# Single table rows addressed in bytes, one unit in 44 fetched so in place of one in 64, and the lanes of two chunks in one broadcast

## The chip, the cores and the metric

The kernel runs on one core of a Trainium2 chip. The metric is the device time of one execution in microseconds (us), as the median of several runs. TensorE (PE), VectorE (DVE), ScalarE (ACT), GpSimd (POOL) and SyncE (SP) each work through their own list of instructions and wait for one another by semaphores. SP does no arithmetic here: it only starts transfers (DMAs).

## The reference

One layer of graph attention over 6,250 nodes and 206,250 edges, 128 features each:

```
n_in, n_out = node[recv], node[send]
e_ij   = leaky_relu(concat([n_in, n_out]) @ W_att + b_att)      # slope 0.2
a_ij   = e_ij @ w_alpha
a_exp  = exp(a_ij - segment_max(a_ij, recv)[recv])
alpha  = a_exp / segment_sum(a_exp, recv)[recv]
n_i    = segment_sum(alpha * (n_out @ W_lin + b_lin), recv)
x      = layernorm(node + elu(n_i))
```

`recv` and `send` are the two ends of each edge. Nodes are handled in 49 blocks of 128.

## The kernel before

**Preparation.** A table `qv_table` in HBM gets one row of 257 numbers (1,028 bytes) for each node: 128 for the sender's part of the hidden layer, 128 for its value, and a one. The edges are sorted by receiver in four parts, and cut into *units* of 128 edges whose receivers lie in one block.

**The loop.** A *chunk* is four units (512 edges), and the loop runs over `NCH` = 415 chunks. For each chunk:

- The 128 table rows of each unit's senders are brought to SBUF. For three units, and mostly for the fourth as well, POOL does this: `gather(k)` issues one indirect DMA per unit (L651) into the ring `rows`, which holds `U` = 8 chunks. A slot comes free when the sums of the chunk eight earlier are done (`high_sums_done`).
- The lanes (the receiver of each edge within its block) come by `lanes_of(k)` on SP (L516): one list of 512 bf16 numbers, broadcast to all 128 partitions, into the ring `lanes_all` of four chunks.
- DVE compares the lanes with the partition number (`make_onehot`, L1530), PE makes the hidden layer (`hidden`, L965 and L967), ACT and DVE the slope and the maximum, PE the scores (`mask`, L977 and L978), DVE the running maxima, ACT the exponentials, PE turns the weights (L985) and sums the weighted rows (`unit_sums`, L993), and DVE adds these to the block's sums (L1581). PE works on the hidden layer of chunk k + 4 while it sums chunk k. Beside this, in about the first 330 chunks, the engines sort the next part of the edges.

**Single rows.** The last unit of every sixteenth chunk (`single_no`; chunks 15, 31, ..., 399, 25 in all) is not gathered by POOL. SP fetches its 128 rows one by one, spread over sixteen chunks: in each chunk `fetch_rows(k)` has one `TENSOR_LOAD` of eight row numbers into registers (L564), and then eight DMAs of one row each, at an address from a register (L569). `hidden(k)` waits for all 128 rows. The numbers in `single_at` are made by DVE; they are row numbers times 257.

**The order of SP's list** is plain: for each chunk `lanes_of(k)`, then `besides(k)` (a few loads and stores for the sort), then `fetch_rows(k)`. `lanes_of(k)` waits until the onehot four chunks earlier is done, which frees its place in the ring.

The rows that are printed for SP name its own list as SPq.

Of the kernel before, what the change touches and what calls it, by code (L numbers as in the profile page):

```python
# [5 lines left out]
F32 = mybir.dt.float32  # L6
BF16 = mybir.dt.bfloat16
I32 = mybir.dt.int32
ALU = mybir.AluOpType
ACT = mybir.ActivationFunctionType  # L10
AX_X = mybir.AxisListType.X

P = 128
# [6 lines left out]
def gnn_kernel(nc, x, src, dst, w_lin, b_lin, w_att, b_att, w_alpha, out):  # L20
# [5 lines left out]
    CHUNK = C * P  # L26
    PER = 4
    UNIT = P
    U = 8
    R = 2 * F + 1  # L30
# [10 lines left out]
    PAD_ROW = NB * P  # L41
# [13 lines left out]
    NO = KEPT // PER  # L55
# [10 lines left out]
    NCH = sum(NCHS)  # L66
# [34 lines left out]
    LANE_RING = 4  # L101


    ROWS_EACH = 8
    ROW_CHUNKS = -(-UNIT // ROWS_EACH)
    RING_S = 2
    COUNTS_S = 4
    def run_ends_of(s):
# [51 lines left out]
    for k in range(NCH):  # L160
# [4 lines left out]
        if k in boundary_at:  # L165
            for kind in ("group", "lows", "old"):
                s = boundary_at[k]
# [6 lines left out]
    TABLE_LAST = [24]  # L174

    table = nc.dram_tensor("qv_table", [(NB + 1) * P, R], F32, kind="Internal").ap()
    flat_table = table.rearrange("n r -> (n r)")
    pads_dram = nc.dram_tensor("pads", [P, PC], F32, kind="Internal").ap()
    sorted_dram = [nc.dram_tensor(f"windows{s}", [WINDOWS, UNIT], F32, kind="Internal").ap() for s in range(OPEN)]
    lanes_dram = [nc.dram_tensor(f"lane_list{s}", [P * W], BF16, kind="Internal").ap() for s in range(SETS)]  # L180

    with ExitStack() as ctx:
# [6 lines left out]
        def sem(name):  # L189
            return ctx.enter_context(nc.semaphore(name))  # L190
# [6 lines left out]
        onesf = sb("onesf", [P, P], F32)  # L197
        part_i = sb("part_i", [P, 1], I32)
        bit_i = sb("bit_i", [P, 1], I32)
        row_sign = sb("row_sign", [P, 1], F32)  # L200
# [11 lines left out]
        sums = sb("sums", [P, NB, F + 1], F32)  # L212
        single_at = sb("single_at", [P, 2, UNIT], I32)
        single_rows = sb("single_rows", [P, RING_S, R], F32)

        keys_i = sb("keys", [P, 2, W], I32)
        keys = keys_i[:].bitcast(F32)
        rows_of = sb("rows_of", [P, W], F32)
        kept = sb("kept", [P, W], F32)
        columns = sb("columns", [P, W], F32)  # L220
        bits = sb("bits", [P, W], I32)
        lane_rows = sb("lane_rows", [P, W], BF16)
        senders = sb("senders", [P, 2, W], I32)
        blocks = sb("blocks", [P, KEPT], I32)
# [53 lines left out]
        lanes_all = sb("lanes_all", [P, LANE_RING, CHUNK], BF16)  # L278
# [4 lines left out]
        rows = sb("rows", [P, U, C, R], F32)  # L283
# [38 lines left out]
        kept_i = kept[:].bitcast(I32)  # L322
# [44 lines left out]
        lanes_made = sem("lanes_made")  # L367
        lanes_ready = sem("lanes_ready")
        lanes_stored = [sem(f"lanes_stored{s}") for s in range(SETS)]
        lanes_in = [sem(f"lanes_in{r}") for r in range(LANE_RING)]  # L370
        unpacked = sem("unpacked")
        blocks_ready = sem("blocks_ready")
        cleared = sem("cleared")
# [20 lines left out]
        onehotT_ready = sem("onehotT_ready")  # L394
# [59 lines left out]
        def place(k):  # L454

            s = min(k // NO, OPEN)
            return s, k - BEGIN[s]
# [4 lines left out]
        def _(sp):  # L462
# [16 lines left out]
            for g in range(PAIRS):  # L479
                n = min(2, NB - 2 * g)  # L480
# [28 lines left out]

            def lanes_of(k):  # L510
                s, n = place(k)
                if k >= LANE_RING:
                    sp.wait_ge(onehotT_ready, k - LANE_RING + 1)
                if n == 0:
                    sp.wait_ge(lanes_stored[s], 16)
                sp.dma_start(lanes_all[:, k % LANE_RING, :],  # L516
                             lanes_dram[s][n * CHUNK:(n + 1) * CHUNK].rearrange("(a e) -> a e", a=1).to_broadcast([P, CHUNK])
                             ).then_inc(lanes_in[k % LANE_RING], 16)

            def besides(k):  # L520
                if k == RAW_AT:
# [30 lines left out]
            def fetch_rows(k):  # L552

                n = k // ROW_CHUNKS
                if n not in single_of:
                    return
                s, row = place(single_of[n])
                first = k % ROW_CHUNKS * ROWS_EACH
                if first == 0:
                    sp.wait_ge(single_ready, s + 1)  # L560
                    if n >= RING_S:
                        sp.wait_ge(high_sums_done, single_of[n - RING_S] + 1)
                for r in range(first, min(first + ROWS_EACH, UNIT), 8):
                    starts = nc.values_load_multi_w_load_instructions(  # L564
                        single_at[row:row + 1, s % 2, r:r + 8], engines=(mybir.EngineType.SP,), min_val=0,
                        max_val=(PAD_ROW + P - 1) * R,
                        skip_runtime_bounds_check_because="they are rows of the table, times the length of a row")[1]
                    for i in range(8):
                        sp.dma_start(single_rows[r + i:r + i + 1, n % RING_S, :],  # L569
                                     flat_table[bass.ds(starts[i], R)].rearrange("(a r) -> a r", a=1)  # L570
                                     ).then_inc(fetched_in(n)[0], 16)

            sp.wait_ge(qv_stored[0], 16 * (PAIRS - PAIRS // 2))
            sp.wait_ge(qv_stored[1], 16 * (PAIRS // 2))
            sp.wait_ge(pad_rows_stored, 16)
            for k in range(NCH):
                lanes_of(k)
                besides(k)
                fetch_rows(k)

# [14 lines left out]
        def _(pool):  # L595
# [7 lines left out]
            for t, one in ((identf, 1.0), (other, 0.0)):  # L603
                g.affine_select(out=t[:], in_=t[:], compare_op=ALU.not_equal, fill=one, base=0,
                                pattern=[[-1, P]], channel_multiplier=1).then_inc(consts, 1)
# [5 lines left out]
            for at in (low, high):  # L611
                g.tensor_tensor(bias_f[at, :], bias_f[at, :], bias_parts[at, :], ALU.subtract).then_inc(bias_split, 1)
            pool.wait_ge(bias_split, 3)
# [464 lines left out]
        def _(dve):  # L1078
            v = nc.vector
# [16 lines left out]
            dve.wait_ge(consts_v, 4)  # L1096
            v.tensor_scalar(row_sign[:], bit_i[:], -2.0, 1.0, ALU.mult, ALU.add).then_inc(consts_v, 1)

# [118 lines left out]
            def find_lanes(s):  # L1217

                if s:
                    dve.wait_ge(lanes_stored[s - 1], 16)  # L1220
                if s < OPEN:
                    dve.wait_ge(kept_in[s], 16)
                    v.tensor_scalar(bits[0:NO, :], kept_i[0:NO, :], SENDER_BITS, P - 1, ALU.arith_shift_right,
                                    ALU.bitwise_and).then_inc(lanes_made, 1)
                    dve.wait_ge(lanes_made, s + 1)
                    v.tensor_copy(lane_rows[0:NO, :], bits[0:NO, :]).then_inc(lanes_ready, 1)
                    if s >= 2:
                        dve.wait_ge(*fetched_in(max(n for k, n in single_no.items() if place(k)[0] == s - 2)))
                    v.tensor_scalar(single_at[0:NO, s % 2, :], kept_i[0:NO, (PER - 1) * UNIT:PER * UNIT], (1 << SENDER_BITS) - 1,
                                    None, ALU.bitwise_and).then_inc(single_found, 1)  # L1230
                    dve.wait_ge(single_found, s + 1)
                    v.tensor_scalar(single_at[0:NO, s % 2, :], single_at[0:NO, s % 2, :], float(R), None,
                                    ALU.mult).then_inc(single_ready, 1)
                else:
                    dve.wait_ge(aside_out, aside_no["rows", s])
                    v.tensor_scalar(kept_i[:], rows_i[:], (1 << SENDER_BITS) - 1, None, ALU.bitwise_and).then_inc(lanes_made, 1)
                    v.tensor_scalar(bits[:], rows_i[:], SENDER_BITS, P - 1, ALU.arith_shift_right,
                                    ALU.bitwise_and).then_inc(lanes_made, 1)
                    dve.wait_ge(lanes_made, s + 1)
                    v.tensor_scalar(lane_rows[:], kept_i[:], float(PAD_ROW), float(P), ALU.is_ge, ALU.mult).then_inc(lanes_made, 1)  # L1240
                    dve.wait_ge(lanes_made, s + 3)
                    v.tensor_tensor(lane_rows[:], lane_rows[:], bits[:], ALU.add).then_inc(lanes_ready, 1)
                    dve.wait_ge(*fetched_in(max(n for k, n in single_no.items() if place(k)[0] == s - 2)))
                    v.tensor_scalar(single_at[:, s % 2, :], kept_i[:, (PER - 1) * UNIT:PER * UNIT], float(R), None,
                                    ALU.mult).then_inc(single_ready, 1)

            def columns_of(s):
# [232 lines left out]
            for run in range(1, runs_of(0)):  # L1480
# [3 lines left out]
                if run % 2:  # L1484
                    stages = phase - LOCAL
                    for h in (0, 1):
                        side = [keys[:, n, h * PIECE:(h + 1) * PIECE] for n in (now, 1 - now)]
                        dve.wait_ge(turn_out, 2 * (run - 1) + h + 1)
                        for n in range(stages):
                            if n:  # L1490
                                dve.wait_ge(compared[0], done)
                            end = n == stages - 1
# [4 lines left out]
                    if run == runs_of(0) - 1:  # L1497
                        dve.wait_ge(run_done[0], 2 * runs_of(0))
                        now = (now + stages) % 2
                        for stage in range(LOCAL - 1, UNIT_BITS - 1, -1):  # L1500
                            if stage < LOCAL - 1:
                                dve.wait_ge(compared[0], done)
                            end = stage == UNIT_BITS
# [20 lines left out]


            def make_onehot(k):
                dve.wait_ge(lanes_in[k % LANE_RING], (k // LANE_RING + 1) * 16)
                if k >= 4:
                    dve.wait_ge(masked_done, k - 3)
                v.tensor_scalar(onehotT[:, k % 4, :], lanes_all[:, k % LANE_RING, :], part_f[:], None, ALU.is_equal, ALU.add,  # L1530
                                accum_out=lane_counts[:, k % 4:k % 4 + 1]).then_inc(onehotT_ready, 1)
# [122 lines left out]
            for g in range(SLICES):  # L1654
                at = slice(g * BY, (g + 1) * BY)
                n = sums[:, at, 0:F]
# [55 lines left out]
```

## Time and profile before

| | |
|---|---|
| median of 3 runs | 2277.44 us (2276.98 to 2277.66) |
| profiled execution | 2278.64 us; from its first instruction to its last 2276.9 us |
| busy | PE 78%, DVE 81%, ACT 65%, POOL 70% of the span |
| DMA | 294 MB, mean 129 GB/s |

Busy shares are averages over the whole span, and issuing a DMA on SP is not counted as busy time of any engine; on POOL it is, since an indirect DMA there is an instruction of the engine.

### The profile page before, as it was taken

What the parts mean: (1) busy time and instruction counts of PE and PEld (TensorE: products, weight loads), DVE (VectorE), ACT (ScalarE), POOL (GpSimd) and SP (SyncE); (2) the same over time, 40 slices, a digit from 0 to 9 for tenths busy, and PEclk for the clock granted to TensorE, in tenths of its full rate; (3) what the DMA queues carried; (4) which work ended last, traced back from release to release, by engine and by line L of the source; (5) the groups of instructions that cost most, each with busy time, mean ns of one, the idle gap of its engine ahead of it and who ended that gap; (6) DMA issues with size and microseconds to landing.
All of it is one profiled execution on the core that took longest, in us unless ns stands there. A gap on an engine that the chain in (4) does not pass through costs nothing.

```text
span 2276.9 us, 63415 instructions
## 1 busy us (share of the span) xinstructions
PE 1779.8 (78%) x11705; PEld 1440.8 (63%) x11705; DVE 1854.8 (81%) x5629; ACT 1471.6 (65%) x4913; POOL 1599.3 (70%) x1670
## 2 busy tenths in 40 slices
PE   5648798888878988887888878888788788877780
PEld 2336676666666766666666666666666666666660
DVE  9849998887789988887898888888767677667667
ACT  2326688876667766665666766676666666666655
POOL 2067777777777777777777777777777777777760
PEclk9869999999999999999999999999999999999995
DMA  3145555555555555555555555555555555555531
GB/s 122 61 113 138 136 138 136 132 133 140 128 135 132 138 133 135 132 138 130 135 132 132 132 138 134 132 136 133 135 137 136 133 137 134 136 134 136 134 105 57
DMA packets 165722, 294.16 MB, mean 129 GB/s; under 512 B 40002, under 2 KB 110014, under 8 KB 165329
## 3 DMA queue, kind: packets, MB, share of 16 engines
q0 software_dynamic: 78864, 216.03, 36.8%
q1 hardware_dynamic: 85733, 73.82, 12.6%
q14 instruction: 292, 2.39, 0.4%
q8 instruction: 101, 1.65, 0.3%
q10 hardware_dynamic: 732, 0.27, 0.1%
HBM read 278.95 MB, written 11.02 MB: 127 GB/s over the span
## 4 chain that ended last, share of the span: by engine, by line
POOL 23%; issue 13%; PE 8%; DVE 5%; DMA 4%; DVEq 1%; ACT 0%; POOLq 0%; ACTq 0%
POOL rows L651 23%; DMA rows<-qv_table,senders 4%; PE hidden_ps L967 2%; PE turned_ps L993 2%; PE masked_ps L978 2%; DVE sums L1581 1%; PE hidden_ps L965 1%; DVE leaky L1537 1%; PE turned_ps L985 1%; DVEq L1581 1%; PE masked_ps L977 0%; DVEq L435 0%; DVE spare L1672 0%; DVE x_sb L1667 0%; DVE keys L1145 0%
## 5 line engine op out<-in xcount | busy, mean ns | idle before, releaser
L651 POOL DMA_INDIRECT rows<-qv_table,senders x1635 | 1571.5, 961 | 498.9 <-issue 471.5
L993 PEld LDWEIGHTS turned_ps<-rows,spare 128*128 128x128 f32 x3270 | 441.8, 191 | 351.3 <-ACT spare L778 207.9
L965 PE MATMUL hidden_ps<-identf,rows 128*128 128x128 f32 x1635 | 461.7, 282 | 257.2 <-DMA rows<-qv_table,senders 242.0
L1581 DVE SCALAR_TENSOR_TENSOR sums<-sums,shrink,turned_ps 128x129 f32 x1660 | 572.7, 345 | 81.4 <-issue 38.4
L763 ACT ACTIVATE spare<-masked_ps,peaks 128x128 f32<-128x128 f32 x1660 | 474.4, 369 | 227.1 <-DVE peaks L1559 225.6
L967 PE MATMUL hidden_ps<-onehotT,p_unit 128*128 128x128 f32 x3320 | 592.4, 280 | 0.0
L993 PE MATMUL turned_ps<-rows,spare 128*128 128x129 f32 x3270 | 481.8, 279 | 114.5 <-DVE sums L1581 108.1
L967 PEld LDWEIGHTS hidden_ps<-onehotT,p_unit 128*128 128x128 f32 x3320 | 523.6, 198 | 0.9 <-issue 0.9
L1544 DVE TENSOR_REDUCE lows<-masked_ps 128x4 f32<-128x512 f32 x415 | 285.6, 688 | 275.9 <-PE masked_ps L978 274.7
L746 ACT ACTIVATE p_unit<-p_all 128x128 f32 x1660 | 400.5, 311 | 74.5 <-issue 50.8
L753 ACT ACTIVATE sloped<-hidden_ps 128x512 f32<-128x512 f32 x415 | 248.9, 600 | 282.8 <-PE hidden_ps L967 278.5
L978 PE MATMUL masked_ps<-leaky,w_cols 128*128 128x512 f32 x830 | 427.5, 596 | 0.0
L965 PEld LDWEIGHTS hidden_ps<-identf,rows 128*128 128x128 f32 x1635 | 237.4, 145 | 298.7 <-issue 283.6
L1530 DVE TENSOR_SCALAR_CACHE_REDUCE onehotT<-lanes_all,part_f 128x512 f32<-128x512 bf16 x415 | 306.8, 739 | 16.3 <-DMA lanes_all<-lane_list 16.0
L1537 DVE TENSOR_TENSOR leaky<-hidden_ps,sloped 128x512 f32<-128x512 f32 x415 | 283.9, 684 | 0.5
L985 PE MATMUL turned_ps<-identf,spare 128*128 128x128 f32 x1660 | 254.9, 277 | 0.0
L778 ACT ACTIVATE spare<-turned_ps 128x512 f32<-128x512 f32 x415 | 247.6, 597 | 4.6 <-PE turned_ps L985 4.3
L1144 DVE TENSOR_TENSOR keys<-keys 128x256 f32<-128x256 f32 (+2 forms) x501 | 195.8, 391 | 14.8 <-ACT keys L700 5.9
L985 PEld LDWEIGHTS turned_ps<-identf,spare 128*128 128x128 f32 x1660 | 201.1, 145 | 0.5 <-issue 0.5
L1145 DVE TENSOR_TENSOR keys<-keys 128x256 f32<-128x256 f32 (+2 forms) x501 | 193.5, 386 | 0.0
L978 PEld LDWEIGHTS masked_ps<-leaky,w_cols 128*128 128x128 f32 x830 | 159.6, 192 | 21.1
L977 PE MATMUL masked_ps<-onehotT,other 128*128 128x512 bf16 x415 | 163.7, 394 | 5.5 <-DVE leaky L1537 5.4
(202 smaller groups left out, 896.5 us busy)
## 6 DMA issues: line engine op xcount, KB each, us to landing
lanes_all<-lane_list SPq DMA_DIRECT2D x415, 128.0 KB
single_rows<-qv_table SPq DMA_DIRECT2D x3200, 1.0 KB
rows<-qv_table,senders POOLq DMA_INDIRECT x1635
qv_table<-rows SPq DMA_DIRECT2D x24, 257.0 KB, 2.7
out<-x_sb SPq DMA_DIRECT2D x1, 1344.0 KB
out<-x_sb SPq DMA_DIRECT2D x1, 896.0 KB
kept<-windows SPq DMA_DIRECT2D x3, 208.0 KB
out<-x_sb SPq DMA_DIRECT2D x1, 448.0 KB
```

What stands on the lines that cost most here:

```text
L651: g.indirect_dma_start(out=rows[:, k % U, c, :], out_offset=None, in_=table, in_offset=bass.IndirectOffsetOnAxis(ap=senders[:, s % 2, c * ...
L746: last = a.activation(p_unit[:, k % 2, c * F:(c + 1) * F], p_all[:, bass.ds(of[c], F)], ACT.Copy)
L763: last = a.activation(weightsT[:, k % 2, unit], masked_ps[:, k % 2, unit], ACT.Exp, bias=peaks[:, at + 2 * n:at + 2 * n + 1])
L965: t.matmul(whole[:, unit], rows_at_unit(k, c)[:, 0:F], identf[:], is_transpose=True, start=True, stop=False, skip_group_check=True)
L967: mm = t.matmul(whole[:, unit], p_unit[:, k % 2, unit], onehotT[:, k % 4, unit], start=False, stop=True, skip_group_check=True)
L978: t.matmul(whole, w_cols[:], leaky[:, k % 2, :], start=False, stop=True).then_inc(masked_done, 1)
L985: mm = t.transpose(weights_ps[:, c * P:(c + 1) * P], weightsT[:, k % 2, c * P:(c + 1) * P], identf[:])
L993: mm = t.matmul(unit_sums_ps[:, c, :], weights[:, k % 2, c * P:(c + 1) * P], rows_at_unit(k, c)[:, F:R], start=True, stop=True)
L1530: v.tensor_scalar(onehotT[:, k % 4, :], lanes_all[:, k % LANE_RING, :], part_f[:], None, ALU.is_equal, ALU.add, accum_out=lane_counts[:, k ...
L1537: v.tensor_tensor(leaky[:, k % 2, :], hidden_ps[:, k % 2, :], sloped[:, k % 2, :], ALU.max).then_inc(leaky_ready, 1)
L1544: v.tensor_reduce(lows_at[:, n * PER:(n + 1) * PER, 1], masked_ps[:, k % 2, :].rearrange("p (i e) -> p i e", i=PER), AX_X, ALU.max, negate ...
L1581: v.scalar_tensor_tensor(out=at, in0=at, scalar=shrink[:, k % 4, i:i + 1], in1=unit_sums_ps[:, i, :], op0=ALU.mult, op1=ALU.add).then_inc( ...
```

## The change

Three things change together. (1) The table is viewed as bytes, `single_at` holds row numbers times 1,028, and each single row is a DMA of 1,028 one-byte elements. (2) A unit is fetched singly every 11 chunks (chunks 10, 21, ..., 406, 37 in all); its 16 loads of eight rows are spread over 11 chunks by `LOADS_TO`, as 1, 1, 2, 1, 2, 1, 2, 1, 2, 1, 2. (3) `lanes_of(k)` runs for even k alone and brings the lanes of two chunks; it waits until the onehot of chunk k - 3 is done, and there are two semaphores of lanes in place of four.

```diff
-    ROW_CHUNKS = -(-UNIT // ROWS_EACH)
+    ROW_CHUNKS = 11
+    LOADS_TO = [-(-UNIT // ROWS_EACH) * n // ROW_CHUNKS for n in range(ROW_CHUNKS + 1)]
...
-    flat_table = table.rearrange("n r -> (n r)")
+    BYTES = R * 4
+    table_bytes = table.bitcast(U8).rearrange("n r -> (n r)")
...
             def lanes_of(k):
                 s, n = place(k)
+                m = min(2, NCH - k)
                 if k >= LANE_RING:
-                    sp.wait_ge(onehotT_ready, k - LANE_RING + 1)
+                    sp.wait_ge(onehotT_ready, k - LANE_RING + m)
                 if n == 0:
                     sp.wait_ge(lanes_stored[s], 16)
-                sp.dma_start(lanes_all[:, k % LANE_RING, :],
-                             lanes_dram[s][n * CHUNK:(n + 1) * CHUNK].rearrange("(a e) -> a e", a=1).to_broadcast([P, CHUNK])
-                             ).then_inc(lanes_in[k % LANE_RING], 16)
+                sp.dma_start(lanes_all[:, k % LANE_RING:k % LANE_RING + m, :].rearrange("p m e -> p (m e)"),
+                             lanes_dram[s][n * CHUNK:(n + m) * CHUNK].rearrange("(a e) -> a e", a=1).to_broadcast([P, m * CHUNK])
+                             ).then_inc(lanes_in[k // 2 % (LANE_RING // 2)], 16)
...
-                first = k % ROW_CHUNKS * ROWS_EACH
+                first, end = [ROWS_EACH * n for n in LOADS_TO[k % ROW_CHUNKS:k % ROW_CHUNKS + 2]]
...
-                for r in range(first, min(first + ROWS_EACH, UNIT), 8):
+                for r in range(first, end, ROWS_EACH):
...
-                    for i in range(8):
-                        sp.dma_start(single_rows[r + i:r + i + 1, n % RING_S, :],
-                                     flat_table[bass.ds(starts[i], R)].rearrange("(a r) -> a r", a=1)
+                    for i in range(ROWS_EACH):
+                        sp.dma_start(single_rows[r + i:r + i + 1, n % RING_S, :].bitcast(U8),
+                                     table_bytes[bass.ds(starts[i], BYTES)].rearrange("(a r) -> a r", a=1)
                                      ).then_inc(fetched_in(n)[0], 16)
...
             for k in range(NCH):
-                lanes_of(k)
+                if k % 2 == 0:
+                    lanes_of(k)
                 besides(k)
                 fetch_rows(k)
...
-                    v.tensor_scalar(single_at[0:NO, s % 2, :], single_at[0:NO, s % 2, :], float(R), None,
+                    v.tensor_scalar(single_at[0:NO, s % 2, :], single_at[0:NO, s % 2, :], float(BYTES), None,
                                     ALU.mult).then_inc(single_ready, 1)
```

The first place is SP's list in the middle of the loop. Before, it repeats one chunk: the lanes, one load, and eight rows, each with an operation on a register ahead of it (moves between registers are not listed here, in either kernel).

```order
L516 DMA lanes_all<-lane_list 128x512
L564 TENSOR_LOAD single_at
L569 REGISTER_ALU
L569 DMA single_rows<-qv_table 1x257
L569 REGISTER_ALU
L569 DMA single_rows<-qv_table 1x257
```

Of the change, SP's list from the lanes of one pair of chunks to those of the next, where three loads stand between them (x8 are eight DMAs in a row).

```order
L520 DMA lanes_all<-lane_list 128x1024
L568 TENSOR_LOAD single_at
L573 DMA single_rows<-qv_table 1x1028 x8
L568 TENSOR_LOAD single_at
L573 DMA single_rows<-qv_table 1x1028 x8
L568 TENSOR_LOAD single_at
L573 DMA single_rows<-qv_table 1x1028 x8
L520 DMA lanes_all<-lane_list 128x1024
```

The operations on registers are gone from between the rows; the lanes stand once for two chunks, with two or three loads behind them in place of one load behind each. In all there are 592 loads and 4,736 rows where there were 400 and 3,200, and 208 broadcasts where there were 415.

The second place is POOL's list of the loop: the gathers (L651) with the scatters of the sort (L633) between them. Before:

```order
L633 DMA windows<-rows_of,place_i 512x128 x4
L651 DMA rows<-qv_table,senders 128x257 x351
L633 DMA windows<-rows_of,place_i 512x128 x4
L651 DMA rows<-qv_table,senders 128x257 x346
L633 DMA windows<-rows_of,place_i 512x128 x4
L651 DMA rows<-qv_table,senders 128x257 x938
```

Of the change:

```order
L638 DMA windows<-rows_of,place_i 512x128 x4
L656 DMA rows<-qv_table,senders 128x257 x348
L638 DMA windows<-rows_of,place_i 512x128 x4
L656 DMA rows<-qv_table,senders 128x257 x344
L638 DMA windows<-rows_of,place_i 512x128 x4
L656 DMA rows<-qv_table,senders 128x257 x931
```

Twelve gathers have left POOL's list (1,635 before, 1,623 now); nothing else in it moved.

## Rows read from the trace of the kernel before

**Rows 1.** The page: busy time of the engines, and the chain that ended last.

```profile
PE 1779.8 (78%) x11705; PEld 1440.8 (63%) x11705; DVE 1854.8 (81%) x5629; ACT 1471.6 (65%) x4913; POOL 1599.3 (70%) x1670
...
POOL 23%; issue 13%; PE 8%; DVE 5%; DMA 4%; DVEq 1%; ACT 0%; POOLq 0%; ACTq 0%
```

**Rows 2.** POOL's gathers, line L651: duration, and what ended the idle time before.

```profile
L651 POOL DMA_INDIRECT rows<-qv_table,senders x1635: 942/949/1577, 129.9 to 2209.3; - x182
...
  issue: 471.5, 1545
  PE turned_ps L993: 27.1, 89
```

**Rows 3.** Timeline of POOL, 1500 to 1520 us: start, length, instruction.

```profile
1500.11 0.95 POOL L651 DMA_INDIRECT rows<-qv_table,senders  x1 [0.30 <-PE turned_ps L993]
...
1519.06 0.95 POOL L651 DMA_INDIRECT rows<-qv_table,senders  x1 [0.30 <-issue]
```

**Rows 4.** SP's waits from 138.2 to 2120 us: total, times, longest.

```profile
SPq L516 <- DVE onehotT L1530: 140.4, 154, 4.6
SPq L537 <- DVE keys L1125: 24.7, 3, 12.0
SPq L546 <- DVE pad_out L1381: 12.2, 1, 12.2
SPq L502 <- DVE lane_rows L1242: 3.9, 1, 3.9
SPq L490 <- DMA windows<-rows_of,place_i: 1.2, 1, 1.2
```

**Rows 5.** SP's instructions by line: shortest/median/longest ns, first and last start.

```profile
L564 SPq TENSOR_LOAD <-single_at x400: 686/727/1059, 138.6 to 2116.4; - x134
L569 SPq ALU_OP  x3200: 32/33/51, 139.4 to 2120.0; - x189
L569 SPq MOVE single_rows<-qv_table x3200: 29/29/42, 139.5 to 2120.1; - x189
L569 SPq DMA_DIRECT2D single_rows<-qv_table x3200: 224/228/312, 139.5 to 2120.1; - x189
L516 SPq DMA_DIRECT2D lanes_all<-lane_list x415: 319/358/363, 138.2 to 2189.3; - x139
```

**Rows 6.** Timelines of SP: the loop's start, its middle, a DMA of the sort, its end.

```profile
138.18 0.36 SPq L516 DMA_DIRECT2D lanes_all<-lane_list  x1
...
1013.21 3.03 SPq L569 DMA_DIRECT2D single_rows<-qv_table  x8
1013.66 0.23 SPq L569 DMA_DIRECT2D single_rows<-qv_table  x1
1016.01 0.23 SPq L569 DMA_DIRECT2D single_rows<-qv_table  x1
1016.29 0.36 SPq L516 DMA_DIRECT2D lanes_all<-lane_list  x1
1017.59 3.03 SPq L569 DMA_DIRECT2D single_rows<-qv_table  x8
...
1027.73 4.78 SPq L496 DMA_DIRECT2D firsts<-windows  x1
...
2120.66 28.09 SPq L516 DMA_DIRECT2D lanes_all<-lane_list  x7
```

**Rows 7.** Busy time of each engine from 1700 to 2200 us.

```profile
core 0: us, PE busy (x) PEld busy (x) DVE busy (x) ACT busy (x) POOL busy (x), PEclk, DMA share, GB/s
...
1700.00:2200.00 500.00, 401.99 (x2752) 331.25 (x2752) 343.31 (x1013) 318.93 (x1118) 378.27 (x400) 0.99 0.53 135
```

**Rows 8.** A DMA's issue with its time to landing; PE's last hidden layer.

```profile
qv_table<-rows SPq DMA_DIRECT2D x24, 257.0 KB, 2.7
...
2213.73 0.27 PE L965 MATMUL hidden_ps<-identf,rows 128*128 128x128 f32 x1
```

**Rows 9.** DVE's waits for lanes over the whole span: total, times, longest.

```profile
DVE onehotT L1530 <- DMA lanes_all<-lane_list: 16.0, 5, 3.9
```

More of the change, by code:

```diff
@@ L8 @@
 I32 = mybir.dt.int32
+U8 = mybir.dt.uint8
 ALU = mybir.AluOpType
@@ L369, in gnn_kernel @@
         lanes_stored = [sem(f"lanes_stored{s}") for s in range(SETS)]
-        lanes_in = [sem(f"lanes_in{r}") for r in range(LANE_RING)]
+        lanes_in = [sem(f"lanes_in{r}") for r in range(LANE_RING // 2)]
         unpacked = sem("unpacked")
@@ L562, in fetch_rows @@
                         sp.wait_ge(high_sums_done, single_of[n - RING_S] + 1)
-                for r in range(first, min(first + ROWS_EACH, UNIT), 8):
+                for r in range(first, end, ROWS_EACH):
                     starts = nc.values_load_multi_w_load_instructions(
-                        single_at[row:row + 1, s % 2, r:r + 8], engines=(mybir.EngineType.SP,), min_val=0,
-                        max_val=(PAD_ROW + P - 1) * R,
-                        skip_runtime_bounds_check_because="they are rows of the table, times the length of a row")[1]
-                    for i in range(8):
-                        sp.dma_start(single_rows[r + i:r + i + 1, n % RING_S, :],
-                                     flat_table[bass.ds(starts[i], R)].rearrange("(a r) -> a r", a=1)
+                        single_at[row:row + 1, s % 2, r:r + ROWS_EACH], engines=(mybir.EngineType.SP,), min_val=0,
+                        max_val=(PAD_ROW + P - 1) * BYTES,
+                        skip_runtime_bounds_check_because="they are rows of the table, times the bytes of a row")[1]
+                    for i in range(ROWS_EACH):
+                        sp.dma_start(single_rows[r + i:r + i + 1, n % RING_S, :].bitcast(U8),
+                                     table_bytes[bass.ds(starts[i], BYTES)].rearrange("(a r) -> a r", a=1)
                                      ).then_inc(fetched_in(n)[0], 16)
@@ L1243, in find_lanes @@
                     dve.wait_ge(*fetched_in(max(n for k, n in single_no.items() if place(k)[0] == s - 2)))
-                    v.tensor_scalar(single_at[:, s % 2, :], kept_i[:, (PER - 1) * UNIT:PER * UNIT], float(R), None,
+                    v.tensor_scalar(single_at[:, s % 2, :], kept_i[:, (PER - 1) * UNIT:PER * UNIT], float(BYTES), None,
                                     ALU.mult).then_inc(single_ready, 1)
@@ L1526, in make_onehot @@
             def make_onehot(k):
-                dve.wait_ge(lanes_in[k % LANE_RING], (k // LANE_RING + 1) * 16)
+                dve.wait_ge(lanes_in[k // 2 % (LANE_RING // 2)], (k // LANE_RING + 1) * 16)
                 if k >= 4:
```

## The prediction

> **What bounds the kernel now.** I read the page first: no engine is over 81% busy, so no mean share names the bound, but the chain that ended last runs through POOL and its issue gaps more than through anything else [rows 1]. So POOL's gathers come next. There are 1,635 of them from 129.9 to 2209.3 us, and the idle time before them is put down to "issue", 1,545 times, which is POOL's own gap; PE's sums, which free a place in the ring, are behind 27 us alone [rows 2]. The timeline shows the even step: from 1500.11 to 1519.06 us lie 15 gathers, 1.26 us each with one longer one among them; 0.95 busy and 0.30 of gap make 1.25 [rows 2, 3]. 1,635 x 1.254 = 2050 of the 2080 us of the loop. POOL runs without a rest: the loop's pace is 4 x 1.254 = 5.02 us a chunk, and 3.76 in each sixteenth.
>
> The second question is how much room SP has, since the change gives SP more. SP's issues are not in the busy shares, so I go to its timeline. One chunk in the middle goes from the first row at 1013.21 to the first row of the next at 1017.59, 4.38 us, with the lanes' DMA only 0.05 us behind the last row, so without any wait [rows 6]. Over the whole loop: the first lanes are issued at 138.18 and those of chunk 400 at 2120.66 us, 1982.5 us for 400 chunks with 400 loads [rows 6]; of these SP waited 182.4 us in all [rows 4], and about 20 went to the sort's other DMAs (one of them 4.78 [rows 6], most about 0.4). That leaves 1780 us, 4.45 a chunk. So SP issues for nine tenths of the time, and its wait is mostly the short one for the onehot that frees a lanes slot [rows 4]. **SP stands 0.5 us a chunk behind POOL's pace as the next bound.**
>
> **What the change costs, part by part.**
>
> *POOL* loses 12 gathers, 12 x 1.254 = 15.0 us. If nothing else becomes the bound the time is 2277 - 15 = 2262. PE has the room for it: 402 us busy in 500 with about 100 chunks, 4.0 us a chunk against 4.88 at the new pace (43 gathers in 11 chunks, 53.9 us) [rows 7].
>
> *SP's price of a row.* From the second row's start (1013.66) to the eighth's (1016.01) are six steps, 0.392 us a row [rows 6]. In it lie three instructions: the operation on a register 0.033, a move 0.029, the DMA's issue 0.228, together 0.290 [rows 5]; 0.102 is between them. The order shows the operation gone. The move I expect to stay: it bears the DMA's own tile names, which the operation does not, it stands once to each such DMA, and lanes, whose address is fixed, have none [rows 5]. So the change saves 0.033 at least and 0.067 with a third of the gaps. I take 0.06, close to the second, since an instruction that is gone can leave no gap of its own. A byte type in place of four bytes changes nothing in the bytes that move, and I cost it at nothing; an issue that gets shorter or longer with it is among the rivals.
>
> *SP's price of a load with its eight rows.* 4.45 less the lanes' 0.40 (0.36 and a gap [rows 5, 6]) is 4.05; less 8 x 0.06 it is 3.57. The `TENSOR_LOAD` in it, 0.727 [rows 5], stays. There are 592 loads in place of 400.
>
> *Lanes.* 208 issues in place of 415. An issue that fills 128 partitions costs 0.36 [rows 5]; with twice the bytes and the same 128 pieces I take the same 0.40 with its gap. That it doubles is the upper bound: 204 x 0.36 = 73 us more in the case where SP is the bound.
>
> *SP in sum.* In 11 chunks 16 x 3.57 + 5.5 x 0.40 = 59.3 us, 5.39 a chunk. POOL needs 4.90 for the same chunk (53.9 / 11). **SP becomes the bound**, by half a microsecond in each of 407 chunks. The two prices cross where a load costs (53.9 - 2.2) / 16 = 3.23, that is where a row gets cheaper by 0.10, half as much again as the operation on the register with its gap.
>
> When SP is the bound nothing makes it wait: POOL runs up to eight chunks ahead, the lanes' slots are free early (the wait of 140 us goes), and the waits for the sort, which arise because SP is ahead of DVE, shrink. So its end is a plain sum from 138.2: 592 x 3.57 = 2113; 204 broadcasts up to chunk 406, 82; other DMAs 20; together 2353. The last rows land some 2.7 us later, if they take as long as the table's stores [rows 8]. Then eight chunks remain, whose gathers POOL has done; they go at PE's pace, 4.2 us (its 4.0 busy and a little) [rows 7], 34 us, to the last hidden layer. Before, that layer began at 2213.7 and the span ended at 2276.9, 63 us later [rows 8], and nothing in that end changes. 2353 + 3 + 34 + 63 = 2453 for the span. The profiled execution took 1.7 us beside its span and was 1.2 above the median, so the median is 2453, 176 us (7.7%) longer.
>
> *The shorter lead of the lanes.* A pair is now asked for one chunk later than its first half was. DVE waited for lanes five times before, 16 us in all [rows 9], so there is a lead; where SP is the bound the lanes come late because SP is late, which is in the sum already.
>
> *The pieces of a row.* An issue that makes 128 pieces takes 0.358 us and one of a single row 0.228 [rows 5], so a piece more costs some 0.001 to issue. The Trainium skill ("DMA: Bandwidth & Descriptors", Why a DMA increments its semaphore by 16 and not by 1) has a DMA split over as many engines, up to 16, as divide its slowest dimension, as the instruction carries it; 257 is prime, 1,028 divisible by 4. By this rule a row addressed in bytes might go as four pieces of 257 bytes, and no row here shows whether it does. By the price of a piece, four in place of one add 0.003 us to a row, 4,736 x 0.003 = 14 us: 2467 in place of 2453. I go by one piece, and keep 2467 among the rivals.
>
> **The rivals.**
>
> *POOL stays the bound, faster.* A row on SP would have to cost 0.29 or less, 0.10 less than now. The mechanism is that the move goes as well: both instructions and two thirds of the gaps, 0.13, make the load 3.01 and SP's chunk 4.58 us, under 4.90. For it speaks that the move may serve the computed offset rather than the DMA; against it that it bears the DMA's names. Then the 12 gathers are the whole difference: 2262, or 2268 where single chunks find their rows late. From 0.10 a row it decides for faster.
>
> *In between.* A row that gets cheaper by 0.07 to 0.10 puts SP between both: 2270 to 2410. In the narrow place where SP costs just what POOL saves, the time is the same.
>
> *Worse than forecast.* The bare 0.033 saved makes the load 3.79 and the time 2581. The same side holds a broadcast whose issue doubles (2526) and, close by, the row in four pieces (2467).
>
> **How the numbers follow.** SP the bound at a price of a row of 0.325 to 0.345: chance 0.66; the load is then 3.51 to 3.67, the time 2418 to 2512, likeliest 2453. POOL the bound: 0.22, at 2262 to 2268. In between: 0.08, of which 0.03 ends as no change. Worse: 0.04. What a measurement of this kernel can tell from no change is about 0.2%, 5 us. Faster 0.23, same 0.03, slower 0.74. The range has to hold 8 in 10, and the likeliest case alone holds 0.66, so it reaches down to the faster one: 2260, and up to 2500, which leaves out the worst and the upper end of the likeliest. The likeliest one's own range is 2410 to 2500.
>
> **What would show it.** Right: in SP's instructions by line no operation but still one move to each row, a step of about 0.33 us between rows, no wait of SP for the onehot, and DVE's onehots or PE's hidden layers waiting for lanes and single rows; chunks of 5.4 us up to chunk 406 and of about 4.2 behind it; POOL waiting for PE's sums in each chunk. Wrong: no move, or a step under 0.29; then SP still waits for the onehot, and POOL's gathers follow one another at 1.25 us to the end.

## The result, and the profile after

The changed kernel takes 2410.66 us (median of 5 runs, 2407.67 to 2411.76) against 2276.98 us of five runs of before: a ratio of 1.0592, 95% interval 1.058 to 1.0604, so 5.9% slower, 134 us. The forecast was 2453, slower, in a range of 2260 to 2500, with 2410 to 2500 as the likeliest case's own. Of the runs below, the medians and ratios leave out one execution of the kernel with 32 row numbers to a load, which took 2586.88 us at a mean granted clock of 0.65 of TensorE, against 0.93 in its others.

The page of the changed kernel, the busy times and the chain that ended last, answers to [rows 1].

```profile
PE 1838.8 (76%) x11705; PEld 1501.1 (62%) x11705; DVE 1848.8 (77%) x5629; ACT 1470.6 (61%) x4913; POOL 1586.4 (66%) x1658
...
SPq 53%; issue 13%; DVE 4%; PE 3%; DVEq 1%; DMA 1%; ACT 0%; ACTq 0%
SPq L573 37%; SPq L568 14%; SPq L520 2%; DVE sums L1586 1%; PE hidden_ps L972 1%; PE masked_ps L983 1%; PE turned_ps L998 1%; DVE leaky L1542 1%; DVEq L1586 0%; DMA lanes_all<-lane_list 0%; PE hidden_ps L970 0%; PE turned_ps L990 0%; DVE spare L1677 0%; SPq L499 0%; DVE x_sb L1672 0%
```

No engine has a larger share than before, and nothing in the busy shares says why the kernel is slower. The chain does: POOL's gathers, 23% of the span before, are gone from it, and 53% of the span is SP's own list, the rows (L573), the loads of row numbers (L568) and the lanes (L520).

SP's instructions by line, shortest/median/longest in ns, first and last start, answer to [rows 5].

```profile
L568 SPq TENSOR_LOAD <-single_at x592: 684/790/1400, 140.0 to 2309.0; - x198
L573 SPq MOVE single_rows<-qv_table x4736: 29/29/42, 140.8 to 2312.1; - x198
L573 SPq DMA_DIRECT2D single_rows<-qv_table x4736: 224/228/505, 140.8 to 2312.2; - x198
L520 SPq DMA_DIRECT2D lanes_all<-lane_list x208: 319/360/376, 139.6 to 2330.4; - x104
```

The operation on a register is gone and the move is there, once to each row. A broadcast of twice the bytes takes 360 ns to issue where one took 358.

Timelines of SP: its first lanes, eight rows of one load with the second and the eighth of them by themselves, the next broadcast and rows, and the end of its loop; they answer to [rows 6].

```profile
139.59 0.36 SPq L520 DMA_DIRECT2D lanes_all<-lane_list  x1
...
506.89 2.52 SPq L573 DMA_DIRECT2D single_rows<-qv_table  x8
507.25 0.23 SPq L573 DMA_DIRECT2D single_rows<-qv_table  x1
509.18 0.23 SPq L573 DMA_DIRECT2D single_rows<-qv_table  x1
509.46 0.36 SPq L520 DMA_DIRECT2D lanes_all<-lane_list  x1
510.69 2.52 SPq L573 DMA_DIRECT2D single_rows<-qv_table  x8
...
2306.42 6.00 SPq L573 DMA_DIRECT2D single_rows<-qv_table  x16
2312.47 18.20 SPq L520 DMA_DIRECT2D lanes_all<-lane_list  x4
```

Six steps from 507.25 to 509.18 are 0.322 us a row; it was 0.392 before. The rows end 192 us later than before, when the last of them was issued just ahead of 2120.66 [rows 6].

Who waits: SP's own waits from 139.6 to 2312 us, then POOL's, DVE's and PE's over the span (total, times, longest); they answer to [rows 2, 4, 9]. The last line is POOL's wait for PE in the kernel before.

```profile
SPq L520 <- DVE onehotT L1535: 1.8, 6, 0.3
SPq L541 <- DVE keys L1130: 0.7, 1, 0.7
...
POOL rows L656 <- issue: 471.3, 1493, 4.3
POOL rows L656 <- PE turned_ps L998: 169.8, 130, 5.9
...
DVE onehotT L1535 <- DMA lanes_all<-lane_list: 260.3, 118, 6.2
PE hidden_ps L970 <- DMA single_rows<-qv_table: 84.5, 34, 4.3
...
POOL rows L651 <- PE turned_ps L993: 27.1, 89, 0.3
```

SP waited 182 us in its loop before, and now waits 2.5 us in 2173: it is saturated. DVE waits 260 us for lanes, 16 before, and PE 84 us for single rows, 34 times, with 37 chunks that have such a unit. POOL waits up to 5.9 us for PE to free a slot of its ring, 0.3 at most before.

### The profile page after: what moved, and what is told of

Same layout as the page of the kernel before. It is cut to its first block, busy times and chain, and to the rows that moved or that the text cites. A ratio compares the mean times of both kernels' runs of the same rounds, so it can differ in the third digit from the quotient of the medians.

```text
span 2410.0 us, 63272 instructions
## 1 busy us (share of the span) xinstructions
PE 1838.8 (76%) x11705; PEld 1501.1 (62%) x11705; DVE 1848.8 (77%) x5629; ACT 1470.6 (61%) x4913; POOL 1586.4 (66%) x1658
## 3 DMA queue, kind: packets, MB, share of 16 engines
q1 hardware_dynamic: 58997, 75.39, 10.7%
## 4 chain that ended last, share of the span: by engine, by line
SPq 53%; issue 13%; DVE 4%; PE 3%; DVEq 1%; DMA 1%; ACT 0%; ACTq 0%
SPq L573 37%; SPq L568 14%; SPq L520 2%; DVE sums L1586 1%; PE hidden_ps L972 1%; PE masked_ps L983 1%; PE turned_ps L998 1%; DVE leaky L1542 1%; DVEq L1586 0%; DMA lanes_all<-lane_list 0%; PE hidden_ps L970 0%; PE turned_ps L990 0%; DVE spare L1677 0%; SPq L499 0%; DVE x_sb L1672 0%
## 5 line engine op out<-in xcount | busy, mean ns | idle before, releaser
L998 PE MATMUL turned_ps<-rows,spare 128*128 128x129 f32 x3246 | 506.6, 284 | 343.6 <-DVE sums L1586 338.4
L972 PE MATMUL hidden_ps<-onehotT,p_unit 128*128 128x128 f32 x3320 | 628.6, 292 | 0.0
L972 PEld LDWEIGHTS hidden_ps<-onehotT,p_unit 128*128 128x128 f32 x3320 | 547.6, 207 | 0.9 <-issue 0.9
L983 PE MATMUL masked_ps<-leaky,w_cols 128*128 128x512 f32 x830 | 439.9, 612 | 0.0
L970 PEld LDWEIGHTS hidden_ps<-identf,rows 128*128 128x128 f32 x1623 | 243.9, 150 | 103.9 <-issue 80.9
L990 PE MATMUL turned_ps<-identf,spare 128*128 128x128 f32 x1660 | 269.2, 288 | 0.0
L990 PEld LDWEIGHTS turned_ps<-identf,spare 128*128 128x128 f32 x1660 | 214.6, 152 | 1.1 <-issue 1.1
L983 PEld LDWEIGHTS masked_ps<-leaky,w_cols 128*128 128x128 f32 x830 | 166.5, 201 | 23.8
L982 PE MATMUL masked_ps<-onehotT,other 128*128 128x512 bf16 x415 | 169.9, 409 | 8.6 <-DVE leaky L1542 8.4
```

The costliest lines, as they stand in the source:

```text
L970: t.matmul(whole[:, unit], rows_at_unit(k, c)[:, 0:F], identf[:], is_transpose=True, start=True, stop=False, skip_group_check=True)
L972: mm = t.matmul(whole[:, unit], p_unit[:, k % 2, unit], onehotT[:, k % 4, unit], start=False, stop=True, skip_group_check=True)
L983: t.matmul(whole, w_cols[:], leaky[:, k % 2, :], start=False, stop=True).then_inc(masked_done, 1)
L990: mm = t.transpose(weights_ps[:, c * P:(c + 1) * P], weightsT[:, k % 2, c * P:(c + 1) * P], identf[:])
L998: mm = t.matmul(unit_sums_ps[:, c, :], weights[:, k % 2, c * P:(c + 1) * P], rows_at_unit(k, c)[:, F:R], start=True, stop=True)
```

## Experiments

Three theories were on record before them. **A**: SP's issues are the bound; the time is the sum of what SP issues up to the last single row, and about 98 us behind it (2410.0 - 2312.5). **B**: the pair of lanes is asked for a chunk later, and DVE's wait for lanes is the cause, not the sign. **C**: the many small transfers hold up the others on the DMA engines. In the diffs the changed kernel is the base.

**Every 16 chunks again**, with bytes and pairs.

```diff
-    ROW_CHUNKS = 11
+    ROW_CHUNKS = 16
```

> The changed kernel with a unit fetched singly every 16 chunks again; bytes and pairs of lanes stay. Theory A (SP's issues are the bound): SP's chunk is one load at 3.50 us (mean of the changed kernel) and half a broadcast at 0.40, 3.70 us, well under POOL's 4.94, and POOL's list is that of before: 2277 us, no change. Theory B (the pair of lanes is asked for a chunk later and DVE waits for it): the pairs are still there, so most of the 134 us stays, over 2350 us. Theory C (the transfers of many single rows hold up the others): as before in number, so 2277 us too.

Measured: 2275.36 us against 2274.64 of before on the same chip, ratio 1.0003 (0.9994 to 1.0012), no change. The pairs alone cost nothing, against B. SP's waits from 140 to 2117 us show where the cheaper issues went, into SP's wait:

```profile
SPq L520 <- DVE onehotT L1535: 457.7, 173, 7.4
```

**Every 13 chunks.**

```diff
-    ROW_CHUNKS = 11
+    ROW_CHUNKS = 13
```

> The changed kernel with a unit fetched every 13 chunks: 31 units, six gathers fewer than before. Theory A: SP's chunk is 16 x 3.50 / 13 + 0.20 = 4.51 us, under POOL's (51 gathers x 1.254) / 13 = 4.92, so POOL is the bound and the time is 2277 - 6 x 1.254 = 2269.5 us. Theory B: over 2350 us. Theory C: 768 rows more than before, half of the 1,536 that cost 134 us, so about 2340 us.

Measured: 2266.89 us against 2274.64 of before on the same chip, ratio 0.9964 (0.995 to 0.9977): 7.75 us less where A said 7.5. 768 rows more than before cost nothing as transfers, against C.

**One chunk's lanes in a broadcast**, every 11 chunks.

```diff
-                m = min(2, NCH - k)
+                m = 1
...
-                if k % 2 == 0:
-                    lanes_of(k)
+                lanes_of(k)
```

(with four semaphores of lanes, as before)

> The changed kernel with one chunk's lanes in a broadcast, as before; bytes and a unit every 11 chunks stay. Theory A: SP issues 203 broadcasts more up to chunk 406, 0.40 us each, 81 us: 2492 us. Theory B: the lead is that of before, so the loss goes: 2262 to 2300 us. Theory C: 2410 us, since the lanes' bytes are the same.

Measured: 2479.55 us (one run), 69 us more than the changed kernel, 12 short of A's sum. The lead of before is back and the kernel is slower, not faster: B falls. The loads account for about that: 394 of them stand right behind lanes in place of 199, where a load is some 0.08 us shorter (last section), 15 us in all. This run does not settle C: the lanes' bytes are the same, but they come in 207 broadcasts more, with 29,808 packets more on SP's queue. The next two experiments leave the packets as they are.

**Rows in four-byte elements**, every 11 chunks, with pairs.

```diff
-                        sp.dma_start(single_rows[r + i:r + i + 1, n % RING_S, :].bitcast(U8),
-                                     table_bytes[bass.ds(starts[i], BYTES)].rearrange("(a r) -> a r", a=1)
+                        sp.dma_start(single_rows[r + i:r + i + 1, n % RING_S, :],
+                                     flat_table[bass.ds(starts[i], R)].rearrange("(a r) -> a r", a=1)
```

(and `single_at` times 257)

> The changed kernel with rows addressed in four-byte elements as before, so with the operation on a register ahead of each row; pairs and a unit every 11 chunks stay. Theory A: a load costs 4.05 us (mean of before) in place of 3.50, 592 x 0.55 = 326 us more: 2736 us. Theories B and C: the same transfers and the same lead, so about 2410 us.

Measured: 2760.69 us (one run), 350 us more, 25 above A's sum. SP's instructions by line of this kernel:

```profile
L573 SPq ALU_OP  x4736: 32/33/54, 140.6 to 2661.9; - x198
L573 SPq MOVE single_rows<-qv_table x4736: 29/29/42, 140.7 to 2662.0; - x198
```

The operation alone, 33 ns, is 156 us over 4,736 rows; 350 / 4,736 = 0.074 us is what one cost with its gap. The transfers have not changed: SP's queue has 58,997 packets and 75.39 MB in both kernels.

**Each DMA brings one row to two partitions**, so 64 DMAs to a unit. The kernel leaves out the odd rows of single units and has copies of the even ones in their place, so its output is not that of the layer; its list of work is otherwise the same.

```diff
-                    for i in range(ROWS_EACH):
-                        sp.dma_start(single_rows[r + i:r + i + 1, n % RING_S, :].bitcast(U8),
-                                     table_bytes[bass.ds(starts[i], BYTES)].rearrange("(a r) -> a r", a=1)
+                    for i in range(0, ROWS_EACH, 2):
+                        sp.dma_start(single_rows[r + i:r + i + 2, n % RING_S, :].bitcast(U8),
+                                     table_bytes[bass.ds(starts[i], BYTES)].rearrange("(a r) -> a r", a=1).to_broadcast([2, BYTES])
```

(and the count that `hidden` waits for is halved)

> The changed kernel, every 11 chunks, but each DMA brings one row to two partitions, so 64 in place of 128 of them to a unit; the odd rows of single units are copies of the even ones, their own are left out. The transfers keep their number of pieces and their bytes. Theory A: SP's load falls from 3.50 by 4 x 0.33 to 2.17 us, its chunk to 3.36, under POOL's 4.90: POOL is the bound and the 12 gathers are saved, 2275 - 15 = 2260 us. Theory C: the same pieces, so about 2410 us.

Measured: 2262.18 us against 2277.26, ratio 0.9935 (0.992 to 0.995): 15.1 us less, the 12 gathers and nothing else. This is the cleanest answer to C. Queue of SP (packets, MB, share) of this kernel; in the changed kernel packets and bytes are the same to the digit.

```profile
q1 hardware_dynamic: 58997, 75.39, 11.4%
```

**Every 12 chunks**, where A has SP and POOL level.

```diff
-    ROW_CHUNKS = 11
+    ROW_CHUNKS = 12
```

> The changed kernel with a unit every 12 chunks: 34 units, nine gathers fewer than before. Theory A (SP's issues against POOL's): SP's chunk is 16 x 3.50 / 12 + 0.20 = 4.87 us, POOL's 47 x 1.254 / 12 = 4.91, so the two are level; 2275 - 9 x 1.254 = 2264 us if SP just keeps up, and up to 2285 where the other DMAs that SP issues for the sort put it behind. Theory C (the transfers of single rows hold up the others): 1,152 rows more than before, about 2375 us.

Measured: 2265.05 us against 2277.26, ratio 0.9944 (0.993 to 0.9957): 12.2 us less. The chain of this kernel has both lists in it, as it should at the crossing:

```profile
POOL 19%; issue 15%; PE 13%; SPq 12%; DVE 8%; DMA 5%; DVEq 2%; ACT 1%; POOLq 0%; ACTq 0%
```

**16 row numbers in a load**, every 11 and every 12 chunks.

```diff
-    ROWS_EACH = 8
+    ROWS_EACH = 16
```

> The changed kernel, every 11 chunks, with 16 row numbers in a TENSOR_LOAD and 16 rows behind it, half as many loads. Theory A: if a load of 16 numbers takes as long as one of eight (0.80 us), 16 rows cost 2 x 3.50 - 0.90 = 6.10 and SP's chunk is 8 x 6.10 / 11 + 0.20 = 4.64 us, under POOL's 4.90: 2260 us. If it takes twice as long nothing is saved but a gap: about 2400 us. The two prices cross at 6.46 us for 16 rows.

> As the last, every 12 chunks. Theory A: SP's chunk is between 8 x 6.10 / 12 + 0.20 = 4.27 and 4.87 us, under POOL's 4.91 at either price of the load of 16 numbers, so 2275 - 9 x 1.254 = 2264 us.

Measured: every 11 chunks 2292.6 us, ratio 1.007 (1.0055 to 1.0086); every 12 chunks 2264.63 us, ratio 0.9945 (0.9932 to 0.9959). The price of the load, by line, in the kernel of 11 chunks:

```profile
L568 SPq TENSOR_LOAD <-single_at x296: 1132/1195/1508, 139.9 to 2186.3; - x148
```

1.195 us lies between the two ends. With it 16 rows cost 7.0 us (two loads of 3.50) less 0.38 (two loads of numbers at 0.79 against one at 1.20) and less a gap, some 6.5 us (in the trace 6.52 in the mean, from a load's start to the end of its last row), and SP's chunk is 8 x 6.5 / 11 + 0.20 = 4.93, by a hair more than POOL's 4.90. So 118 of the 134 us are back, and SP is still the bound (61% of the span in the chain that ended last).

**32 row numbers in a load**, every 11 chunks (`ROWS_EACH = 32`).

> The changed kernel, every 11 chunks, with 32 row numbers in a TENSOR_LOAD and 32 rows behind it. Theory A: loads of 8 and of 16 numbers took 0.79 and 1.20 us, so 0.05 a number; one of 32 should take 2.0, and 32 rows with it 2.1 + 32 x 0.33 = 12.7 us. SP's 11 chunks cost 4 x 12.7 + 2.2 = 53.0 us against POOL's 53.9: 2277 - 15 = 2262 us by the means. A rival speaks of order and not of means: 12.7 us in one go keep the next broadcast of lanes behind them, longer than their lead, so DVE waits for lanes in four chunks of eleven, and the time is 2275 to 2300 us.

Measured: 2295.73 us against 2279.47, ratio 1.0065 (1.0049 to 1.0081). The sum of A said 2262 and is wrong here; the rival's 2275 to 2300 holds. A piece of SP's timeline, and the waits of PE, DVE and SP over the span, of this kernel:

```profile
1506.79 0.35 SPq L520 DMA_DIRECT2D lanes_all<-lane_list  x1
1509.34 10.70 SPq L573 DMA_DIRECT2D single_rows<-qv_table  x32
1520.09 1.93 SPq L520 DMA_DIRECT2D lanes_all<-lane_list  x2
...
PE hidden_ps L970 <- DMA single_rows<-qv_table: 129.5, 34, 9.1
DVE onehotT L1535 <- DMA lanes_all<-lane_list: 114.4, 35, 9.8
...
SPq L520 <- DVE onehotT L1535: 62.9, 34, 14.0
```

From one broadcast to the next lie 13.3 us, 2.7 chunks at POOL's pace, in which SP brings no lanes, and a broadcast brings two chunks' lanes. At other times SP itself waits for a lanes slot, 45 of the 63 us inside its loop, so it is not short of time in the mean. The mean of SP's issues fits; their order does not.

**Lanes of four chunks in a broadcast**, every 11 chunks, 16 numbers to a load, a ring of eight.

```diff
-    LANE_RING = 4
+    LANE_RING = 8
...
-    ROWS_EACH = 8
+    ROWS_EACH = 16
...
-                m = min(2, NCH - k)
+                m = min(4, NCHS[s] - n)
...
-                if k % 2 == 0:
+                if k % 4 == 0:
```

(with two semaphores of lanes, one for each four chunks)

> The changed kernel, every 11 chunks, 16 row numbers to a load (2292.6 us by itself), and the lanes of four chunks in one broadcast, into a ring of eight. Theory A: SP's 11 chunks cost 8 x 6.52 + 2.75 x 0.40 = 53.3 us in place of 54.4, against POOL's 53.9, so POOL is just the bound: 2262 us, or up to 2275 with the sort's other DMAs. If an issue takes longer for twice the bytes, 0.40 more in 104 of them is 42 us over the loop, and nothing is gained against 2292.

Measured: 2265.69 us against 2279.47, ratio 0.9935 (0.9922 to 0.9947): 0.40 us less in each four chunks takes the kernel of 11 chunks from 0.7% slower to 0.65% faster. The ring of eight lets SP bring lanes earlier as well; SP's waits for a slot in the loop were only 2.7 us without it, so the fewer issues are the larger part. The broadcast of 4 KB to a partition takes no longer to issue (L520 of this kernel):

```profile
L520 SPq DMA_DIRECT2D lanes_all<-lane_list x104: 357/363/427, 140.4 to 2163.3; - x104
```

This one, every 12 chunks (with 8 or with 16 numbers to a load) and every 13 beat both kernels, by 0.4 to 0.65%. The intervals of the first three overlap, so no order among them is shown.

## Why the prediction was right, and where its size was off

**SP becomes the bound: shown.** SP's waits fell from 182 to 2.5 us, and each experiment that changes the number or price of SP's issues moved the time by about that sum, up or down, with 32 numbers to a load as the exception, where the order counts; four-byte rows and one row to two partitions did so at the same packets and bytes on SP's queue, which leaves nothing to C.

**The price of a row was set too high.** The term that was mis-sized is "I take 0.06" for what the register's operation costs with its gap. The step between rows fell from 0.392 to 0.322, so by 0.070, and four-byte rows put it at 0.074 over all rows: the operation took a whole gap with it and a little of the next. A second term erred the other way: the `TENSOR_LOAD`, said to stay at 0.727, took 0.790 in the median (0.05 more in the mean, last section), and gave part of this back. With lanes and other DMAs at the prediction's own prices, SP's load is in the mean (2312.47 - 139.59 - 204 x 0.40 - 20 - 2.5) / 592 = 3.495 us, where 3.57 was forecast: 0.075 x 592 = 44 us. A start 1.4 us later and 2.5 us of waits take 4 of these back, so the rows end at 2312.5 where 2353 was forecast; the other 3 of the miss of 43 us lie behind them.

**The likeliest case held by a hair.** The saving of 0.070 lies beyond the 0.067 that the prediction gave as its upper figure, and at the border of its case "in between", which began at 0.07. The likeliest case's sum reached down to 2418; only the margin with which its range was stated as 2410 takes in 2410.66. The mechanism was right; that the likeliest range still holds the time is in part luck, since a row at 0.322 lies outside the 0.325 to 0.345 that it stood for, and the longer loads made up for some of it.

**The rest of the sum held.** PE's hidden layer of chunk 406 and the last one, which answers to [rows 8]:

```profile
2313.58 0.45 PE L970 MATMUL hidden_ps<-identf,rows 128*128 128x128 f32 x1 [2.43 <-DMA single_rows<-qv_table]
2315.52 0.42 PE L970 MATMUL hidden_ps<-identf,single_rows 128*128 128x128 f32 x1
...
2346.79 0.27 PE L970 MATMUL hidden_ps<-identf,rows 128*128 128x128 f32 x1
```

PE waited for the single rows and went on 1.1 us behind the end of SP's rows (3 forecast). Eight chunks took 33.2 us (34 forecast), and the end behind the last hidden layer 2410.0 - 2346.8 = 63.2 (63). Broadcasts of twice the bytes cost the same to issue, as taken. The pace of 4.88 us a chunk set beside PE's 4.0 should be the 4.90 of 53.9 / 11, which changes nothing. One sign did not come: POOL was to wait for PE's sums in each chunk, and it did so 130 times in 415 chunks.

**The move stays: shown**, so the rival that POOL stays the bound fell with its condition. What it would give was right too: where SP's price was brought under POOL's in other ways (one row to two partitions), the 12 gathers gave 15 us. The crossing was forecast at 3.23 us a load for 11 chunks, 6.46 for 16 rows: 16 rows at some 6.5 us are just above it, and SP is the bound. For 12 chunks the same sum gives (47 x 1.254 - 12 x 0.20) / 16 = 3.53 us; the load of 3.50 is just below it, and the nine gathers were saved.

**A row in four pieces: refuted here.** The Trainium skill's rule ("DMA: Bandwidth & Descriptors", Why a DMA increments its semaphore by 16 and not by 1) goes by the slowest dimension "as the instruction carries it". The packets on SP's queue, of before and of the changed kernel:

```profile
q1 hardware_dynamic: 85733, 73.82, 12.6%
```

```profile
q1 hardware_dynamic: 58997, 75.39, 10.7%
```

Two experiments give the packets of one DMA, one chunk's lanes in a broadcast and every 16 chunks:

```profile
q1 hardware_dynamic: 88805, 75.40, 12.1%
```

```profile
q1 hardware_dynamic: 55925, 73.80, 11.3%
```

The first has 207 broadcasts more than the changed kernel and 29,808 packets more, 144 to each; the second has 1,536 rows fewer and 3,072 packets fewer, two to each. That fits 128 pieces and 16 packets for the semaphore to a broadcast, and one and one to a row. With these, 415 x 144 + 3,200 x 2 leaves 19,573 of the packets before for all else, and 208 x 144 + 4,736 x 2 leaves 19,573 of the changed kernel's. A byte row is one packet of data, as a row of four-byte elements was; the experiment with four-byte rows has the same 58,997. So the 1,028 is not a dimension that splits in this instruction.

**The lanes' shorter lead**, costed at nothing, was nothing: every 16 chunks, with pairs, is level with before. That DVE waits 260 us for lanes in the changed kernel is the sign of a late SP.

## What to carry to other kernels

An engine that only issues DMAs has no busy share in these profiles, and can be the next bound all the same: add up its issues for one round of the loop from its timeline, gaps and register instructions with them, before work is moved to it. Here nine tenths of SP's time was taken, the change gave it 48% more rows and made each row's step only 18% cheaper, and a saving of 15 us became a loss of 134; one chunk more between the units (12 in place of 11) turns the same code into a gain of 12 us. And where such an engine is nearly full, the order counts beside the sum: long runs of its issues keep back the short one that others wait for.

## What the runs showed that I had not expected

A load of row numbers takes longer behind single-row DMAs than behind a broadcast. Two loads of the changed kernel, by line, in windows of their own: the first follows rows, the second lanes.

```profile
L568 SPq TENSOR_LOAD <-single_at x1: 809/809/809, 506.0 to 506.0; - x1
...
L568 SPq TENSOR_LOAD <-single_at x1: 733/733/733, 509.9 to 509.9; - x1
```

These two are no exception: in the trace of the changed kernel the mean is 0.726 us for the 199 loads right behind lanes and 0.805 for the 380 right behind rows. Before, 387 of 400 loads stood behind lanes, and the median was 727 ns; in the changed kernel two of three stand behind rows, and it is 790. Why is open. A load of 16 numbers took 1,195 ns, and 32 took 2,106 (L568 of the kernel with 32 numbers to a load):

```profile
L568 SPq TENSOR_LOAD <-single_at x148: 2026/2106/2511, 139.5 to 2181.9; - x148
```

From the three medians I estimate 0.05 to 0.06 us a number on a base of some 0.3 to 0.4.

Beside a late SP, TensorE's clock is lower: from 1700 to 2200 us the granted clock was 0.94 (the line below) against 0.99 of before [rows 7]. After the wait of 2.43 us for single rows the products from 2313.5 to 2316.0 us ran at a granted clock of 0.50, the lower level of 1.2 GHz (0.45 and 0.42 us at 2313.58 and 2315.52 above); from 2346.7 to 2349.0 it was 1.00 (0.27 us at 2346.79). The sum of SP's issues accounts for the time without it; no run here changes the clock by itself.

```profile
1700.00:2200.00 500.00, 389.13 (x2539) 324.13 (x2538) 319.12 (x950) 290.34 (x1031) 350.62 (x370) 0.94 0.47 126
```
